# First feed-forward chunk woven into the last attention tiles, layer norms in one ScalarE pass, x's first tile loaded alone

## The reference

```
x = x + layernorm(attention(layernorm(x)))    # 32 query heads, 8 key/value heads of 128, causal
x = x + layernorm(ffn(layernorm(x)))
attention: qkv = q @ w_qkv.T; softmax(q k^T / sqrt(128)) v per head; @ w_dense.T
ffn: g = Q(x) @ W1.T; u = Q(x) @ W3.T; h = silu(g) * u; y = Q(h) @ W2.T    # inner width 1792
Q(a): divides each block of 128 columns by its scale max|a|/448 + 1e-12, and multiplies by it again
W1, W3, W2: weights times one scale for each block of 128x128
```

## Time and profile before

| | |
|---|---|
| median of 3 runs | 1252.56 us (1251.1 to 1252.85) |
| profiled execution: time, span | 1252.92 us, 1251.1 us |
| TensorE busy | 1218.0 us, 97% |
| VectorE busy | 798.3 us, 64% |
| ScalarE busy | 613.5 us, 49% |
| GpSimd busy | 701.3 us, 56% |
| mean granted TensorE clock | 0.994 of full speed |

### The profile page before, as it was taken

The page is one execution under the profiler, slowest core; times in us unless marked ns, Lnnn a source line. Parts: engine busy times, 40 slices in busy tenths (PEclk is TensorE's granted clock), DMA queues, the critical chain, the costliest instruction groups (busy, mean ns, idle before and its releaser), DMA issues.

```text
span 1251.1 us, 18084 instructions
## 1 busy us (share of the span) xinstructions
PE 1218.0 (97%) x6184; PEld 1008.2 (81%) x6184; DVE 798.3 (64%) x1945; ACT 613.5 (49%) x1364; POOL 701.3 (56%) x818
## 2 busy tenths in 40 slices
PE   8999999999999999999999999999999899999996
PEld 7888888888888888888888888888877678888885
DVE  4644544466676666666766766767777865565568
ACT  5433243256666666656666666656656621111111
POOL 6744555334735645536535536537555687767645
PEclk9999999999999999999999999999999999999999
DMA  5444553330020020020120210200400101011101
GB/s 204 139 164 168 193 202 135 135 127 26 27 84 26 26 91 28 17 93 26 45 67 25 89 31 26 90 21 26 143 18 1 51 4 61 39 51 50 50 0 67
DMA packets 59457, 89.74 MB, mean 72 GB/s; under 512 B 3440, under 2 KB 44400, under 8 KB 56048
## 3 DMA queue, kind: packets, MB, share of 16 engines
q1 hardware_dynamic: 58800, 87.65, 20.1%
q10 hardware_dynamic: 576, 1.05, 0.2%
HBM read 61.43 MB, written 27.26 MB: 71 GB/s over the span
## 4 chain that ended last, share of the span: by engine, by line
PE 87%; DVE 5%; ACT 4%; POOL 2%; issue 1%; DMA 1%; ACTq 0%; POOLq 0%; DVEq 0%
PE psS L1069 25%; PE psOY L1181 16%; PE psOY L1069 14%; PE psOY L1196 12%; PE psT L1069 10%; PE psT L1165 9%; DVE pT_lo L789 1%; PE psS L1217 1%; DVE probs L846 1%; ACT pT_hi L644 1%; ACT probs L649 1%; DVE oT_lo L789 1%; ACT oT_hi L753 1%; DVE st L792 0%; DMA raw<-in_w_v 0%
## 5 line engine op out<-in xcount | busy, mean ns | idle before, releaser
L433 POOL TENSOR_SCALAR probs<-probs,rsum 128x512 f32<-128x512 f32 (+7 forms) x256 | 193.6, 757 | 348.3 <-DVE rsum L853 345.5
L789 DVE TENSOR_TENSOR pT_lo<-psT,pT_hi 128x512 fp32r<-128x512 f32 (+3 forms) x384 | 211.9, 554 | 78.0 <-ACT pT_hi L644 75.1
L649 ACT ACTIVATE probs<-probs,negmax 128x512 f32<-128x512 f32 (+7 forms) x256 | 199.6, 780 | 55.5 <-DVE negmax L846 54.5
L644 ACT CAST pT_hi<-psT 128x512 fp32r<-128x512 f32 (+3 forms) x384 | 182.3, 477 | 75.0 <-PE psT L1165 74.6
L1165 PE MATMUL psT<-ident,probs 128*128 128x128 f32 x1152 | 192.3, 276 | 8.3 <-DVE pT_lo L789 8.0
L846 DVE CUSTOM_DVE_ANT_0 probs<-psS,mask 128x512 f32<-128x512 f32 (+7 forms) x256 | 192.1, 751 | 5.1 <-PE psS L1069 3.7
L1165 PEld LDWEIGHTS psT<-ident,probs 128*128 128x128 f32 x1152 | 142.8, 141 | 62.3 <-DVE pT_lo L789 32.5
L1069 PE MATMUL psS<-kT_hi,qT_hi 128*128 128x512 f32 (+2 forms) x384 | 152.4, 397 | 0.0
L1069 PE MATMUL psS<-kT_hi,qT_lo 128*128 128x512 f32 (+2 forms) x384 | 132.0, 344 | 0.0
L1069 PE MATMUL psS<-kT_lo,qT_hi 128*128 128x512 f32 (+2 forms) x384 | 131.3, 342 | 0.0
L1181 PE MATMUL psOY<-pT_hi,v_hi 128*128 128x512 f32 x288 | 118.8, 412 | 0.8 <-DVE pT_lo L789 0.7
(11 more groups left out here) (141 smaller groups left out, 2655.0 us busy)
## 6 DMA issues: line engine op xcount, KB each, us to landing
qT_lo<-q_scr SPq DMA_DIRECT2D x64, 256.0 KB, 2.8
raw<-in_w_qk SPq DMA_DIRECT2D x10, 1024.0 KB, 5.6
q_scr<-cB SPq DMA_DIRECT2D x16, 512.0 KB, 2.6
q_scr<-cA SPq DMA_DIRECT2D x16, 512.0 KB, 2.7
raw_wd<-in_w_dense SPq DMA_DIRECT2D x8, 1024.0 KB, 7.8
raw_up<-in_w_up SPq DMA_DIRECT2D x7, 1024.0 KB, 4.8
v_scr<-vout SPq DMA_DIRECT2D x16, 256.0 KB, 2.4
kT_lo<-k_scr SPq DMA_DIRECT2D x8, 512.0 KB, 4.1
```

The lines of the kernel that those rows point to most:

```text
L433: nc.gpsimd.tensor_scalar(probs[:, h, 0:cols], probs[:, h, 0:cols], rsum[:, h:h + 1], 1.0, ALU.mult, ALU.mult).then_inc(p_ready, 1)
L644: nc.scalar.copy(dst, src).then_inc(t_hi, 1)
L649: nc.scalar.activation(row, row, ACT.Exp, bias=negmax[:, h:h + 1], scale=-1.0, accum_out=lsum[:, h:h + 1]).then_inc(e_done, 1)
L789: return nc.vector.tensor_tensor(dst, source, hi.bitcast(F32), ALU.subtract)
```

## The change

In group 7 the norms get new items: `SY` (statistics and root of the projected tile), `OY` (offset -mean*root on VectorE), `NY` (one ScalarE pass with scale and offset), `RX` (residual and its statistics, then the root), `OX`, `NX` (offset and pass for x1), `QX` (scales, quantising), and `X1` (the turn of the new activation, from step 3 on). The first chunk's weights (`W` 0 to 3) are loaded to another place (`raw_up0`) and split in group 6, `W` 4 and 5 in steps 2 and 3 of group 7. The last step and the whole first chunk are one list, `end_items`, with `GU`, `H`, `TH`, `DN` for gate and up, hidden tile, its turn, and down; `W1` are the second chunk's pieces. In the finish a norm is an offset on VectorE and a pass on ScalarE (`norm_fin`); GpSimd adds one tile later than before. At the start SP alone issues the loads, x's tile 0 first, and ScalarE runs a small copy ahead of its first work; `warm` runs 30 and 10 times and no longer 24 and 8.

```diff
 def step_items(t):
...
+            if last and s >= 2:
+                items += [[("NY", s - 2)], [("RX", s - 2)], [], [("OX", s - 2)]][h]
+            if last and s >= 3 and h == 1:
+                items.append(("X1", s - 3))
...
         if t >= 1:
             items.append(("A", t - 1))
-        if last:
-            if 1 <= s <= KT or s >= NT - CB:
-                items.append(("W", s - 1 if s <= KT else KT + s - (NT - CB)))
-            items += [(kind, s - lag) for kind, lag in (("stat_y", 1), ("root_y", 1), ("root_x1", 2), ("quantise", 4))
-                      if s >= lag]
+        if last and s >= 1:
+            items.append(("SY", s - 1))
+        if last and s >= 2:
+            items += [("NX", s - 2), ("QX", s - 2)]
+        if g == G - 2 and s < KT:
+            items.append(("W", s))
+        if last and 2 <= s < 2 + CB:
+            items.append(("W", KT + s - 2))
...
         items.append(("O", t))
+        if last and s >= 1:
+            items.append(("OY", s - 1))
...
+    def end_items():
+
+        t = T - 1
+        assert ORDER[NT - 1] == TPB and C >= 2
+        return [("P", t, 0, 0), ("NY", 5), ("GU", 0), ("Y", t - 1, 0), ("P", t, 0, 1), ("RX", 5), ("Y", t - 1, 1),
+                ("P", t, 0, 2), ("H", 0), ("Y", t - 1, 2), ("P", t, 0, 3), ("OX", 5), ("Y", t - 1, 3), ("A", t - 1),
+                ("X1", 4), ("NX", 5), ("P", t, 1, 0), ("SY", 6), ("P", t, 1, 1), ("QX", 5), ("PV", t, 0),
+                ("P", t, 1, 2), ("PV", t, 1), ("P", t, 1, 3), ("OY", 6), ("GU", 1), ("PV", t, 2), ("NY", 6),
+                ("PV", t, 3), ("PV", t, 4), ("O", t), ("RX", 6), ("TH", 0), ("GU", 2), ("H", 1),
+                *(("Y", t, h) for h in range(HG)), ("A", t), ("SY", 7), ("OX", 6), ("NX", 6), ("TH", 1), ("X1", 5),
+                ("GU", 3), ("QX", 6), ("H", 2), ("OY", 7), ("NY", 7), ("DN", 0), ("TH", 2), ("W1", 0), ("GU", 4),
+                ("RX", 7), ("H", 3), ("DN", 1), ("TH", 3), ("X1", 6), ("W1", 1), ("GU", 5), ("OX", 7), ("NX", 7),
+                ("H", 4), ("DN", 2), ("QX", 7), ("TH", 4), ("W1", 2), ("GU", 6), ("H", 5), ("DN", 3), ("TH", 5),
+                ("W1", 3), ("X1", 7), ("DN", 4), ("GU", 7), ("H", 6), ("DN", 5), ("TH", 6), ("W1", 4), ("H", 7), ("W1", 5)]
...
-            for i in range(5):
+            load_x(0)
+            load_values_weight(0)
+            load_values_weight(1)
+            load_x(1)
+            load_values_weight(2)
+            load_values_weight(3)
+            for i in range(2, 5):
                 load_x(i)
...
-                if t == T - NT + 2:
-                    sp.wait_ge(wd_ready, G * HG)
-                    sp.dma_start(raw_up[:], w_up[0]).then_inc(ffn_in, 16)
+                if t == T - 2 * NT:
+                    sp.dma_start(raw_up0[:], w_up[0]).then_inc(ffn_in, 16)
                     sp.dma_start(raw_down[:], w_down[0]).then_inc(ffn_in, 16)
...
-            for n in range(NT):
-                quantise_hidden(n, n % 2)
-                if n < 3:
-                    quantise_tile(NT - 3 + n)
...
-                if n == 1:
-                    pool.wait_ge(ffn_in, 64)
-                    pool.wait_ge(o_full, T)
-                if 1 <= n <= PIECES:
-                    prepare(1, 1, n - 1)
+                elif kind == "H":
+                    quantise_hidden(args[0], args[0] % 2)
+                elif kind == "W1":
+                    if args == [0]:
+                        pool.wait_ge(ffn_in, 64)
+                        pool.wait_ge(t_full, TURN["P", T - 1, 1, HG - 1] + 1)
+                    prepare(1, 1, *args)
...
-            def center(dst, src, negmean, s, stat):
-                act.wait_ge(stat, s + 1)
-                nc.scalar.activation(dst, src, ACT.Identity, bias=negmean[:, s:s + 1]).then_inc(centered, 1)
...
+            def norm_y(s):
                 tile = y[:, ORDER[s], :]
+                act.wait_ge(offset_y, s + 1)
+                nc.scalar.activation(tile, tile, ACT.Identity, bias=nmean[:, s:s + 1],
+                                     scale=rstd[:, s:s + 1]).then_inc(yn_ready, 1)
...
+            act.wait_ge(const_ready, 1)
+            nc.scalar.copy(half[:, 1:2], half[:, 0:1])
...
+            def offset(negmean, means, rs, s, root, done):
+
+                dve.wait_ge(root, s + 1)
+                nc.vector.tensor_scalar(negmean[:, s:s + 1], means[:, s, 0:1], rs[:, s:s + 1], -1.0, ALU.mult,
+                                        ALU.mult).then_inc(done, 1)
...
-            warm(24)
+            warm(30)
             turn_x(0)
-            warm(8)
+            warm(10)
```

More of the change, by code:

```diff
@@ L61, in p_banks @@
         return (ORDER[t % NT] + TPB) // TPB
-    NORMS = [[("center_y", 2), ("scales", 4)], [("norm_y", 2)], [("center_x1", 3), ("residual", 2)],
-             [("norm_x1", 3), ("stat_x1", 2)]]
     PIECES_KV = 4
     def step_items(t):
-        s, g, items, following, two = t % NT, t // NT, [], t < T - 1, p_banks(t) == 2
+        s, g, items, two = t % NT, t // NT, [], p_banks(t) == 2
         last = g == G - 1
@@ L71, in step_items @@
             shares = [[], [], [], []]
-        elif not two:
-            shares = [[], [0], [1], [2, 3]]
-        else:
-            shares = [[], [0], [1], []] if following else [[], [0, 1], [], [2]]
-        exps = [("E", t + 1, h) for h in range(HG) if following]
+        else:
+            shares = [[], [0], [1], []] if two else [[], [0], [1], [2, 3]]
+        exps = [("E", t + 1, h) for h in range(HG)]
         for h in range(HG):
-            items.append(("P", t, 0, h))
-            if following:
-                items.append(("S", t + 1, h))
+            items += [("P", t, 0, h), ("S", t + 1, h)]
             if h >= 1:
@@ L186, in sandwich_kernel @@
         rstd, rstd1, nmean, nmean1 = (small(n, [P, NT]) for n in ("rstd", "rstd1", "nmean", "nmean1"))
-        half = small("half", [P, 1])
+        half = small("half", [P, 2])
         amax, qs, qr = (small(n, [P, 2, KT]) for n in ("amax", "qs", "qr"))
@@ L254, in turned @@
         def turned(item):
+            if item[0] == "X1":
+                return [tile_of(u, ORDER[item[1]]) for u in xn1T]
             _, t, b, h = item
@@ L372, in inverse_root @@
                 pool.wait_ge(stat, i + 1)
-                nc.gpsimd.tensor_tensor(rs[:, i:i + 1], means[:, i, 1:2], half[:], ALU.pow).then_inc(done, 1)
+                nc.gpsimd.tensor_tensor(rs[:, i:i + 1], means[:, i, 1:2], half[:, 0:1], ALU.pow).then_inc(done, 1)
             def low(dst, source, hi):
@@ L581, in _ @@
             feed_forward_chunk(C - 1, 0, False)
-            for s in (NT - 2, NT - 1):
+            for s in (NT - 2, NT - 1, NT):
                 finish(s)
@@ L742, in _ @@
                 kind, *args = item
-                if kind == "P":
+                if kind in ("P", "X1"):
                     hi_of_turn(item)
@@ L775, in _ @@
                     hi_of_hidden(n - 1, (m - 1) % 2)
+            for m in range(2 * NT):
+                n = (C - 2) * NT + m
+                silu_gate(n, m % 2)
+                hi_of_hidden(n - 1, (m - 1) % 2)
+                if m - 4 >= NT:
+                    norm_fin(m - 4 - NT)
             hi_of_hidden(C * NT - 1, (C * NT - 1) % 2)
+            for s in range(NT - 4, NT):
+                norm_fin(s)
         @block.vector
@@ L989, in _ @@
                 kind, *args = item
-                if kind == "P":
+                if kind in ("P", "X1"):
                     lo_of_turn(item)
+                    if kind == "X1" and args[0] >= NT - 2:
+                        link(nc.vector.memset(y[:, ORDER[args[0]], :], 0.0))
                 elif kind == "S":
@@ L1056, in _ @@
                 if m - 2 >= NT:
-                    finish(m - 2 - NT)
-            for s in (NT - 2, NT - 1):
-                add_down((C - 1) * NT + s, s, False)
-                finish(s)
-            finish(NT)
+                    finish_statistics(m - 2 - NT)
+                if m - 3 >= NT:
+                    finish_offset(m - 3 - NT)
+            add_down((C - 1) * NT + NT - 2, NT - 2, False)
+            finish_statistics(NT - 2)
+            finish_offset(NT - 3)
+            add_down((C - 1) * NT + NT - 1, NT - 1, False)
+            finish_statistics(NT - 1)
+            finish_offset(NT - 2)
+            finish_offset(NT - 1)
+            i = ORDER[NT - 1]
+            dve.wait_ge(z_ready, NT)
+            nc.vector.tensor_tensor(x1[:, i, :], x1[:, i, :], y[:, i, :], ALU.add).then_inc(last_ready, 1)
         @block.tensor
```

230 lines of the change are left out of this document (84 added, 146 removed).

## The result

The changed kernel takes 1266.24 us (median of 4 runs, 1264.79 to 1267.23) against 1252.69 for the kernel before (4 runs, 1251.1 to 1252.85): ratio 1.011, 95% interval 1.0093 to 1.0128. It is 13.6 us slower, where 2.9 faster was forecast. The profiled executions have spans of 1265.0 and 1251.1 us, so the trace has 13.9 us to explain.

A forecast was written before the change was run, and what follows sets the result against it. TensorE, busy 97% of the span, was taken as the bound, so only removing its waits pays. 1.3 + 3.8 + 2.8 - 4.2 - 0.8 = 2.9 us gained gave 1249.7 us, range 1241 to 1255.

The forecast's parts named there:

- Part 2: Last tile and first feed-forward chunk: 44.9 us of work plus 9.2 of stalls, 54.3 against 57.1, gain 2.8.
- Part 1: Attention steps 3 to 6 of the last group: 46.4 us against 50.25, stalls of 3.9 included, gain 3.8.
- Part 3: Second chunk: its weight pieces, one hidden tile later on GpSimd, delay the next loads and hidden tile 9; loss 4.2 us.
- Part 4: Start: x's first tile lands near 3.5 us, first product at 9.3 to 9.5 and not 10.60; gain 1.3 us.
- Part 5: Finish: the norm as VectorE offset, later ScalarE pass and the same add; loss 0.8 us.
- B: Rival, last tile through second chunk: weaving covers the work, part 3's loss and some 3 us of stalls go; 1242.5, chance 0.30.
- C: Rival, norms: VectorE waits in its own queue for GpSimd's roots, 8.8 us lost; 1258.5, chance 0.10.
- D: Rival, middle of kernel: the clock sinks after the stalls of 3.2 and 4.2, 3.4 us go; 1253.1, chance 0.18.

The follow-up runs named there:

- filled kernel: The changed kernel with TensorE doing transposes nobody reads in its waits (last tile's step, ahead of hidden turns 2, 5 and 9): 1260.79 us.
- the start alone: The kernel before with only the changed kernel's start (loads, warm-up, ScalarE order): 1250.22 us, against 1252.16 for the kernel before beside it.
- repaired: The changed kernel with VectorE's work spread, SiLU table loaded early, second chunk's pieces earlier and H2 ahead of q's scales: 1254.61 us.
- a lone wait of 3.6 us: The kernel before with the new start, plus one added TensorE wait on GpSimd in group 6: 1255.42 us, against 1250.22 without it.

## Why the prediction was wrong

**Part 2 failed most** (gain 2.8 forecast, loss 5.6 measured): 62.66 where the sum had 54.3. The filled kernel parts the miss of 8.4. With the clock at 1.00 the stretch is 58.77, so 3.9 are the clock behind waits. The sum priced the dense work at 0.227 for each matmul from the earlier trace rows, which holds at full clock only; I had read in the earlier trace rows that 0.90 goes with waits of 1 to 2 us, but made it a rival, and gave it there to the waits of 3.2 and 4.2 alone. The second failed term is the stalls. In the filled kernel TensorE's fills of this stretch take 0.71 + 0.93 + 1.04 + 0.93 + 2.79 + 2.56 = 8.96 and its waits 3.58, some 12.5 in place of the 9.2 forecast, 3.3 more. (The changed kernel's waits add up to only 10.3: behind the slow matmuls tile 3's turn doesn't wait there.) The dense rest of 46.2 is 1.1 over 44.9 and the 0.2 of rounding. Of the single stalls, tile 5's 3.2 was 2.87, but tile 2's 1.7 was 3.14, and the table load of 1.28 was not in the sum at all.

Tile 2's chain of 6.4 us (accumulation to quantised tile) took 8.1, from 999.87 to 1007.97. The timelines of ScalarE and VectorE show a link that the sum lacks:

```profile
1001.85 0.82 ACT L676 ACTIVATE y<-x,nmean,rstd 128x512 f32<-128x512 f32 x1 [4.32 <-DVE nmean L807]
...
1002.96 0.42 DVE L797 TENSOR_TENSOR hT_lo<-psS,hT_hi 128x256 fp32r<-128x256 f32 x1 [1.14 <-ACT hT_hi L691]
```

ScalarE stands before a norm's pass until VectorE has made the offset, and the casts that VectorE itself needs next are queued behind that pass. No run moves this pass alone, so its price isn't shown.

By the Trainium skill (ScalarE: Activation LUTs, What ACT_TABLE_LOAD costs) a switch of tables is a load of about 1.28 us and a drain of about 1.38. The load agrees with the trace's 1.28; the drain doesn't show: the row ahead ends at 977.42 and the load begins at 977.43, and the first SiLU begins 0.02 behind its end.

**Part 1 failed** (gain 3.8, loss 2.7). The stalls of 3.9 were 1.29 + 0.51 + 1.58 + 1.29 + 0.52 + 0.90 + 1.21 = 7.3. The low clock in step 3 is no loss of its own: in the filled kernel, whose fills lie elsewhere, these steps had a clock of 1.00, and took 52.71 all the same, with one more wait of 1.03 for the new activation's low part. So the stalls at full clock are 8.3, 4.4 over the forecast, and 1.9 of dense work are missing in a sum made from steps without waits. Of that 1.9, some 1.4 isn't the change's: the start alone, at a clock of 1.00, has 6.45 of waits in these steps and 42.1 of dense work, where the steps of group 6 gave 40.7. The waits for the new activation's low part were priced at 1.2 and 1.1 in the two-bank steps, and were 1.03 (at full clock) and 0.90; in the others they were priced at 0.5 and 0.6, and were 1.58 and 1.21. The projection's wait for the output's low part, in the sum with 0.5 in step 5 alone, was 1.29 in both two-bank steps, and each turn of the new activation there waits 0.5 for GpSimd's quantising, which has no term in the sum. VectorE's timeline of step 4 shows the longest of these waits:

```profile
940.87 1.54 DVE L881 TENSOR_TENSOR x<-x,y 128x512 f32<-128x512 f32 x1
942.45 0.69 DVE L800 BATCH_NORM_STATS2 st<-x 128x6 f32<-128x512 f32 x1
...
943.47 0.68 DVE L797 TENSOR_TENSOR xn1T_lo<-psT,xn1T_hi 128x512 fp32r<-128x512 f32 x1
944.06 0.41 DVE L797 TENSOR_TENSOR pT_lo<-psT,pT_hi 128x256 fp32r<-128x256 f32 x1
```

and beside the first of them, on GpSimd, a weight piece:

```profile
940.58 1.28 POOL L400 TENSOR_TENSOR down_lo<-raw_down,down_hi 128x512 fp32r<-128x512 f32 x1
```

The residual takes 1.54 where it took 0.68 in the earlier trace rows. In the four steps VectorE is busy 44.5 us, 38.0 before. One other order of this work left the steps as long (53.20), and with three turns fewer the waits still add up to 6.6, which points at VectorE's total work; no run takes work off VectorE alone, so that stays an argument. By the Trainium skill (SBUF — State Buffer, Who interferes with whom) a VectorE operation with both inputs in SBUF contends with a GpSimd operation that reads SBUF; the residual agrees, and 0.67 is its time again at 953.65, beside no piece. The prediction used this rule for the finish alone and had counted the residual at its lone time.

**Part 3 was right in its mechanism and size**, 4.2 forecast and a wait of 4.21 measured, with each link as described. What it lacked is the clock behind the wait, 0.71 over 9.2 us; filled, the rest is 2.2 shorter (227.2 for 229.4), and 4.2 + 2.2 is nearly the loss of 6.55. With the pieces one tile earlier the rest is 224.0: 5.4 of 7.0 come back, and tile 9 still waits 1.31.

**Part 4 was right** (gain 1.3 forecast, 1.34 measured; the start alone gives 1.9 on the medians). The tile landed at 3.34 and the product started at 9.99, not at 9.3 to 9.5, since the turn began at 7.47 and not 7.1. That is 0.6 sooner than before, and step 3 begins 1.34 sooner; the other 0.7 is not explained, and lies within the microsecond of chance in one profile. **Part 5** was right in sign: loss 0.46 for 0.8. Its mechanism was another. The offset at 1259.00 took 0.21 beside GpSimd's add, not stretched, and VectorE's final add took 0.69 beside the last of GpSimd's. The prediction had drawn from the Trainium skill (SBUF — State Buffer, Who interferes with whom) that the final add would wait too; here it was GpSimd's add beside it that took longer, some 1.7 of the 2.97 for two, where others take 1.26. That add, one tile later than before, ends the kernel, and not ScalarE's pass with VectorE's add.

**The rivals.** B needed another order of the items: repaired, the stretch is 1.6 under the kernel before, but the time never comes near 1242.5. C as written is not seen: in steps 3 to 6 no offset of the changed kernel waits for a root, and the one at the finish waits 0.54. But the wait is handed on: ScalarE waits for offsets, 1.86 and 1.87 us in the two-bank steps and 4.32 at tile 2. D was the right mechanism, worth 0.18 to me and priced at 3.4 us. The windows above lack some 10.4 us of clock in five places; filling gave 5.5 back. The others didn't lengthen the kernel: steps 3 to 6 took 52.71 at full clock too, and behind tile 2 the next turn then waits 1.34 for GpSimd. Of the 16.8 us between forecast and profile, some 6 are the clock behind waits (3.9 in part 2, 2.2 in part 3), 7.7 are stalls that were too small or not in the sum (4.4 in part 1, 3.3 in part 2), and 3.0 are dense work that the sum was short of.

## What to carry to other kernels

Price a wait of TensorE with the granted clock behind it: a lone wait of 3.6 us cost 5.2 here, and behind several waits near 1 us in a row the clock fell too, though not in every profile. Before weaving work into a busy stage, add it up for the queue that is fullest there (VectorE here, 44.5 us busy in four steps, 38.0 before). A piece of background work put one item later in GpSimd's queue can cost more than the whole weaving brings. Of a bundle, time the parts: here the start alone gains 1.9 us, and the rest, even repaired, gives none and may take that gain away again.

## What the runs showed that was not expected

- After nearly the same waits the clock fell in one kernel and not in another: steps 3 to 6 have 0.90 in two windows of the earlier trace rows, and 1.00 with the start alone, whose waits there are the same (1.28, 0.94, 1.22, 0.93). That is 1.7 us between profiles of the same code, so the 2.68 that steps 3 to 6 lost against the earlier trace rows would be 4.4 against the other profile.
- What a wait costs in clock differs: behind the lone one of 3.63, the clock was 0.54 over 3.0 us and 0.92 over the next 4.0 (to 852.80), 1.7 us missing; behind one of 3.14 it was 0.50 over 5.7 (1007.90 to 1013.60), 2.9 missing. What decides this the runs don't show.
- Transposes that nobody reads made the changed kernel 5.5 us faster, and cost 0.9 where there was no wait to fill.
